# Four attention layers: two banks of sums in turn and a ring of two banks for the second self-attention layer

## The reference

```python
def _forward(x, encoder_out, norm_w, Wq, Wkv, Wqf, Wkf, Wwin, Wout):
    xn = rmsnorm(x, norm_w)
    q = (xn @ Wq).reshape(B, T_dec, H, hd)
    k, v = ...                       # (encoder_out @ Wkv): 77 tokens of context
    q_phi = taylor_feature_map(q @ Wqf)
    k_phi = taylor_feature_map(k @ Wkf)
    kv_state = jnp.einsum('bshf,bshd->bhfd', k_phi, v)
    linear_out = jnp.einsum('bthf,bhfd->bthd', q_phi, kv_state)
    normalizer = jnp.einsum('bthf,bhf->bth', q_phi, k_phi.sum(axis=1))[..., None]
    linear_out = linear_out / (normalizer + EPS_DEN)
    kv_win = (xn @ Wwin).reshape(B, T_dec, 2, H, hd)
    scores = jnp.einsum('bthd,bshd->bhts', q, k_win) * (1.0 / math.sqrt(hd))
    allowed = (j <= i) & (j >= i - WINDOW)
    probs = softmax(where(allowed, scores, min))
    window_out = jnp.einsum('bhts,bshd->bthd', probs, v_win)
    return residual + concatenate([linear_out, window_out]) @ Wout
```

## Time and profile before

| | us |
|---|---|
| Median of 3 runs | 2349.58 |
| Lowest and highest run | 2344.32, 2349.96 |
| Profiled execution, its own time | 2344.72 |
| Its span in the trace | 2343.0 |
| TensorE busy (share of the span) | 2060.6 (88%) |
| TensorE's weight loads | 1351.1 (58%) |
| VectorE busy | 1409.6 (60%) |
| ScalarE busy | 1132.0 (48%) |
| GpSimd busy | 728.3 (31%) |

### The profile page before, as it was taken

One profiled execution on the slowest core, in us unless ns is written; L12 is line 12 of the kernel. 1 busy time (PEld: TensorE's weight loads), 2 busy tenths in 40 slices (PEclk: granted clock), 3 DMA queues, 4 the chain that ended last, 5 costly groups with the idle time before them and its releaser, 6 DMA issues. The chain is left out here.

```text
span 2343.0 us, 38173 instructions
## 1 busy us (share of the span) xinstructions
PE 2060.6 (88%) x14594; PEld 1351.1 (58%) x14594; DVE 1409.6 (60%) x3047; ACT 1132.0 (48%) x1675; POOL 728.3 (31%) x817
## 2 busy tenths in 40 slices
PE   4898999899998879887889898996989995899989
PEld 2333433343343268775565575664677773888989
DVE  5775776586678356635535454451577882656655
ACT  1255465555555756523434534362555553545444
POOL 2013114113213143311524426153110100555656
PEclk8799999999999989998999999999999996999999
DMA  6705404502530000036440805302222212000000
GB/s 129 144 6 108 57 1 75 88 8 51 91 72 1 1 14 1 10 90 89 112 58 29 141 1 122 48 2 79 81 82 95 82 42 72 6 14 13 12 14 19
DMA packets 77772, 126.65 MB, mean 54 GB/s; under 512 B 16652, under 2 KB 34828, under 8 KB 77584
## 3 DMA queue, kind: packets, MB, share of 16 engines
q1 hardware_dynamic: 74968, 122.63, 25.0%
q10 hardware_dynamic: 2624, 1.58, 0.2%
HBM read 93.59 MB, written 30.32 MB: 53 GB/s over the span
## 5 line engine op out<-in xcount | busy, mean ns | idle before, releaser
L1007 DVE TENSOR_REDUCE nmx_causal<-banks 128x1 f32<-128x333 f32 (+4 forms) x896 | 436.0, 537 | 174.9 <-PE banks L739 172.1
L893 ACT ACTIVATE probs_causal<-banks 128x1024 f32<-128x1024 f32 (+3 forms) x384 | 352.4, 952 | 283.0 <-PE banks L764 279.9
L739 PE MATMUL banks<-ks_causal,qs_causal 96*128 96x333 bf16 (+4 forms) x896 | 272.8, 342 | 11.8 <-DVE nmx_causal L1007 9.5
L670 POOL TENSOR_SCALAR_AFFINE_SELECT probs_window<-probs_window 128x512 f32<-128x512 f32 (+1 forms) x272 | 162.8, 605 | 306.7 <-ACT probs_window L893 296.2
L670 POOL TENSOR_SCALAR_AFFINE_SELECT probs_causal<-probs_causal 128x512 f32<-128x512 f32 x128 | 89.0, 696 | 510.4 <-ACT probs_causal L893 510.4
L764 PE MATMUL banks<-qs_causal,ks_causal 97*128 97x512 bf16 (+4 forms) x896 | 220.1, 343 | 28.1 <-DMA qs_causal<-nmT_causal 15.0
L1007 DVE TENSOR_REDUCE nmx_window<-banks 128x2 f32<-128x384 f32 (+2 forms) x320 | 140.5, 458 | 117.2 <-PE banks L739 115.5
L788 PE MATMUL banks<-probs_causal,v_causal 128*17 128x512 f32 (+4 forms) x1792 | 198.6, 516 | 0.0
L893 ACT ACTIVATE probs_window<-banks 128x768 f32<-128x768 f32 (+2 forms) x128 | 99.8, 783 | 129.3 <-PE banks L764 128.8
L739 PEld LDWEIGHTS banks<-ks_causal,qs_causal 96*128 96x128 bf16 x896 | 87.2, 100 | 111.8 <-DVE nmx_causal L1007 70.4
L737 PEld LDWEIGHTS banks<-below,identb 128*128 128x128 bf16 x512 | 50.3, 99 | 168.1 <-DVE nmx_causal L1007 116.9
(11 more groups left out here) (251 smaller groups left out, 4098.6 us busy)
## 6 DMA issues: line engine op xcount, KB each, us to landing
fs_masked<-in_fside SPq DMA_DIRECT2D x32, 616.0 KB, 3.7
ks_causal<-zk SPq DMA_DIRECT2D x96, 137.6 KB
ks_window<-zk SPq DMA_DIRECT2D x96, 137.6 KB
qs_causal<-zq SPq DMA_DIRECT2D x96, 128.0 KB
qs_window<-zq SPq DMA_DIRECT2D x96, 128.0 KB
zk<-parts_causal SPq DMA_DIRECT2D x24, 275.2 KB, 2.5
zk<-parts_window SPq DMA_DIRECT2D x24, 275.2 KB, 2.4
zq<-parts_causal SPq DMA_DIRECT2D x24, 256.0 KB, 4.6
```

The lines of the kernel that those rows point to most:

```text
L670: pool.affine_select(out=v, in_=v, compare_op=ALU.is_ge, fill=0.0, base=const, pattern=[[0, QH], [by_c, wd]], channel_multiplier=by_p).the ...
L739: ins = pe.matmul(bk[:, c:c + m], qs[q][0:KR, h, t * P:(t + 1) * P], ks[q][0:KR, h, key:key + m], start=cover is None, stop=True, skip_gro ...
L893: ins = act.activation(dst, src, ACT.Exp, scale=DH ** -0.5)
L1007: dve.tensor_reduce(dst, src, AX.X, ALU.max, negate=True).then_inc(emptied_v, 1)
```

## The change

The windowed layer gets two banks of sums, 6 and 7, used by its turns alternately; the causal layer keeps bank 6 alone. A turn's first multiply waits for the copy of the turn before the last. In return bank 7 leaves the ring for all tokens of layers 1 and 2: their ring has banks 0 and 1, and a fill waits for the fill two back. For the causal layer the ring stays 0, 1, 7. The class Ring now takes a function from token to banks, goes through each choice of banks by turn, and remembers for each fill the last user of its bank. VectorE clears both banks before the layer. On every engine the instructions keep their order; VectorE has one memset more.

```diff
     def __init__(self, banks, where, order, emptier, ready, done):
-        self.banks, self.where, self.emptier, self.ready = banks, where, emptier, ready
+        self.banks, self.ready, self.done = banks, ready, done
         tokens = [t for t in order if emptier(t)]
-        self.done = done
         self.at = {t: n for n, t in enumerate(tokens)}
-        count, self.counts = dict.fromkeys(done, 0), []
-        for t in tokens:
+        count, turn, last = dict.fromkeys(done, 0), {}, {}
+        self.counts, self.used, self.before = [], [], []
+        for n, t in enumerate(tokens):
             count[emptier(t)] += 1
             self.counts.append((done[emptier(t)], count[emptier(t)]))
+            choice = where(t)
+            bank = choice[turn.get(choice, 0) % len(choice)]
+            turn[choice] = turn.get(choice, 0) + 1
+            self.used.append(bank)
+            self.before.append(last.get(bank))
+            last[bank] = n
...
     def wait_free(self, pe, token):
-        n = self.at[token] - len(self.where)
-        if n >= 0:
+        n = self.before[self.at[token]]
+        if n is not None:
             pe.wait_ge(*self.counts[n])
...
-PAIRS, OUT = (2, 4), 6
+PAIRS, SUMS = (2, 4), {True: (6,), False: (6, 7)}
...
+    sums_of = lambda n: SUMS[first][n % len(SUMS[first])]
...
+                out = sums_of(turn_number[b, q, c])
                 if s == 0:
-                    n = turn_number[b, q, c]
-                    if n:
-                        pe.wait_ge(out_copied, n)
+                    n = turn_number[b, q, c] - len(SUMS[first])
+                    if n >= 0:
+                        pe.wait_ge(out_copied, n + 1)
                     else:
-                        pe.wait_ge(cleared, 2)
+                        pe.wait_ge(cleared, 1 + len(SUMS[first]))
...
-                        ins = pe.matmul(banks[32 * h:32 * h + DH + 1, OUT, query:query + n],
+                        ins = pe.matmul(banks[32 * h:32 * h + DH + 1, out, query:query + n],
...
-                act.activation(oT[:, k % 2, :], banks[:, OUT, :], ACT.Copy).then_inc(out_copied, 1)
+                act.activation(oT[:, k % 2, :], banks[:, sums_of(k), :], ACT.Copy).then_inc(out_copied, 1)
...
-                dve.memset(banks[:, OUT, :], 0.0).then_inc(cleared, 1)
+                for bank in SUMS[first]:
+                    dve.memset(banks[:, bank, :], 0.0).then_inc(cleared, 1)
...
-    shared = Ring(banks, (0, 1, 7), order, emptied_by, sem("ring_ready"), {"v": sem("emptied_v"), "s": sem("emptied_s")})
+    shared = Ring(banks, lambda token: (0, 1) if token[0] else (0, 1, 7), order, emptied_by, sem("ring_ready"), {"v": sem("emptied_v"), "s": sem("emptied_s")})
```

More of the change, by code:

```diff
@@ L394, in __init__ @@
     def __init__(self, banks, where, order, emptier, ready, done):
-        self.banks, self.where, self.emptier, self.ready = banks, where, emptier, ready
+        self.banks, self.ready, self.done = banks, ready, done
         tokens = [t for t in order if emptier(t)]
-        self.done = done
         self.at = {t: n for n, t in enumerate(tokens)}
-        count, self.counts = dict.fromkeys(done, 0), []
-        for t in tokens:
+        count, turn, last = dict.fromkeys(done, 0), {}, {}
+        self.counts, self.used, self.before = [], [], []
+        for n, t in enumerate(tokens):
             count[emptier(t)] += 1
             self.counts.append((done[emptier(t)], count[emptier(t)]))
+            choice = where(t)
[4 more added lines that the diff above has]
+            last[bank] = n
     def bank(self, token):
-        return self.banks[:, self.where[self.at[token] % len(self.where)], :]
+        return self.banks[:, self.used[self.at[token]], :]
     def filled(self, token):
@@ L941, in step @@
             if token == ("ring", 0, 0, 0, 0):
-                dve.wait_ge(cleared, 2)
+                dve.wait_ge(cleared, 1 + len(SUMS[first]))
             if emptier(token) == "v":
@@ L1240, in front_layers @@
     names = [lambda s, tag=tag: sem(f"{s}_{tag}") for tag in ("causal", "ff", "window")]
-    shared = Ring(banks, (0, 1, 7), order, emptied_by, sem("ring_ready"), {"v": sem("emptied_v"), "s": sem("emptied_s")})
+    shared = Ring(banks, lambda token: (0, 1) if token[0] else (0, 1, 7), order, emptied_by, sem("ring_ready"), {"v": sem("emptied_v"), "s": sem("emptied_s")})
     rings = [Own(shared, n) for n in range(3)]
     products_of = lambda token: {"up": "s", "down": "v"}.get(token[0])
-    own_banks = Ring(banks, (2, 3, 4, 5, 6), of(1), products_of, sem("product_ready"),
+    own_banks = Ring(banks, lambda token: (2, 3, 4, 5, 6), of(1), products_of, sem("product_ready"),
                      {"v": sem("product_emptied_v"), "s": sem("product_emptied_s")})
```

## The result

The change made the kernel slower: 2405.88 us against 2349.77 (medians of 4 runs each, 2402.98 to 2407.23 and 2344.32 to 2351.80). The ratio is 1.0233, 95% interval 1.0214 to 1.0252. That is 56 us lost where +32.5 was summed up and 2380 forecast, and it lies above the range's 2398.

A forecast was written before the change was run, and what follows sets the result against it. TensorE was taken as the layer's bound. On the profiled 2344.7 us, -15 + 13 + 18 + 2 + 2.5 + 12 = +32.5 gave 2377; half of the median's 5 us excess on top made 2380 us, range 2352 to 2398.

The forecast's parts named there:

- Part 1: Second bank of sums in the windowed layer's attention: TensorE no longer waits for ScalarE's copy, -15 us, bounds 10 to 19.6.
- The cap by the transposes: Attention turns: where transposes of the copied sums follow a stall, at most 0.55 us of it comes back.
- Value stages: Ring of two where values are projected: each next value block waits 0.41 us, 3.3 us a batch, 13 us for four.
- Feed-forward layer: Ring of two at 820 to 1050 us: none of 33 fills begins before the bank two back is free, 0 us.
- Output stages: Ring of two: 18 us over the first three batches' output stages, 2 us in the last batch's.
- The three places of one passage: First three output stages: waits of 0.59, 0.41 and 0.26 us add up to 1.26 us a passage, five passages a stage.
- The stage of maxima alone: 1055 to 1065 us, once: about 0.1 us more for each of 20 fills, 2.5 us, between 0 and 3.3.
- Attention stages: Ring of two: late fills cost 12 us, 3 a batch, bounds 0 and 19.4; TensorE's idle time absorbs part.
- the walk: Fill-by-fill count of delays with two ring banks, no idle time taken off; 19.4 us in the attention stages.
- Rival 4: Slower by more, 2395 us and up: walk's full cost of 57, gain only 10; lower clock can add; chance 0.15.
- Two banks enough: Rival 2: the ring of two costs nothing, only the second bank of sums acts, 2330 or 2325 us; chance 0.08.
- Cancel: Rival 3: the gain of the second bank and the ring's loss cancel, 2344 to 2355 us; chance 0.15.

The follow-up runs named there:

- e1: The changed kernel with only one bank of sums everywhere, the ring of two kept in the feed-forward and windowed layers: 2417.70 us, ratio 1.0297 to the kernel before.
- e3: Kernel before, with two alternating banks of sums only in each batch's last five turns and a ring of two only there: 2343.59 us, ratio 0.9973.
- e7: The kernel of e3 measured again on another chip with more runs: 2349.02 us, ratio 0.9991 to the kernel before.
- e4: e1 plus filler multiplies with unused results before three waits in each of three batches: 2411.49 us, ratio 1.0263 to the kernel before.
- e5: Kernel before, one bank of sums, ring of two only in the second group of heads of the first three batches: 2381.84 us, ratio 1.0128.

## Why the prediction was right or wrong

**Direction: right, and for the stated reason.** The ring of two costs more than the second bank gives.

**Part 1: right.** 15 us forecast, 12 by the medians of e1 and the change, 15 by their traces, of which 9 are idle time; the rest is most likely in part the clock. The cap by the transposes holds: their row of waits for the copy grew from 3.2 to 8.5 us. Waits for GpSimd's masks, which I had not priced, took 3 us more (5.5 against 2.5).

**Value stages: right.** 13 forecast, 13.3 measured, 3.3 a stage, with the step of 0.41 us seen: value blocks follow each other after 1.64 us (1250.07 to 1251.71), and after 1.23 before.

**Feed-forward layer: put at 0, some 3 us measured.** "None of its 33 fills begins before the bank two back is free" left out the place where the ring changes. The first layer's last fills use three banks in turn and the feed-forward layer's first already two, and there the bank that comes next needn't be the one used two fills back. Shown is the wait of 2.11 us at 817.71; that the order of banks makes it is my reading.

**Output stages: right in kind, two sizes off.** In the first three 18 was forecast and 13.6 came (13.6 to 16.2 in the kernels with a ring of two there). The three places of one passage don't all bind each time: of 15 passages, 12 show a wait of a block of maxima for ScalarE's copy (5.3 us), 12 one for VectorE's addition (2.7), and 3 one of the transpose for the maxima (1.1). In the last one 2 was forecast and 4.3 came. All of the 4.3 is counted as busy time, and the lower level lasts 6.1 us longer there; e3 and e7, with three ring banks in this stage, are 1.4 longer at 3.4 us more of it. That is a term I didn't have. Its first product, eight multiplies that take 1.89 to 1.97 us before, takes 3.75 at a granted clock of 0.50:

```profile
1656.13:1659.88 3.75, 3.75 (x10) 2.93 (x10) 0.00 (x0) 0.60 (x1) 0.00 (x0) 0.50 0.00 0
```

**The stage of maxima alone:** 2.5 forecast, 3.1 after, 1.6 to 2.6 in the other kernels with a ring of two there. The size is right, but TensorE stands at the lower level for 9.9 us more there and is busy 2.9 us more, so the trace doesn't show whether the mechanism I had or the clock makes the 3.1.

**Attention stages: the step that failed.** 12 us forecast and 40 measured with a ring of two alone (e1), of which 29.6 lie in the three stretches with projections. Outside of these it is 10.4 us, which the 12 would have covered. Inside, the prediction said that "part of the delay falls into waits that end when they end, such as one where VectorE is held for 2.60 us by a cast". It took such long holds by a third engine as time that would swallow delays. At the place that it named, in the third group, that was so: TensorE's longest wait there is 2.16 us before and 2.84 after, and all four third groups lose only 0.8 us by idle time (the other 4.2 of their 5.1 are busy time, with 10.2 us more of the lower level). In the second group the holds are the opposite. A hold of a bank by ScalarE that waits for GpSimd is itself a bank taken out of the ring, for 4.5 us. With three banks two were left to go on with; with two only one is, and TensorE stops at once. And the end of the hold isn't fixed: it moves along with TensorE. From the start of the held fill to ScalarE's copy of it, it is 5.76 us before (1282.69 to 1288.45) and 5.57 after (1312.67 to 1318.24), while the stretch has grown. By the recorded times alone the fill behind it lacked 3.9 us (1285.13 to 1289.05), in one of three such stretches; the whole walk of the prediction came to 19.4 us for all sixteen groups, and even this upper bound is under the 29.6 of the three. How much of it the walk gave to these fills is not on record.

**The clock: named, not priced, and expected elsewhere.** Rival 4 looked for the lower level behind the new gaps of the value and output stages. The value stages have 0.5 us more of it, the first three output stages 3.0. Where it came is the projection stretches (20.5), the third groups (10.2), the stage of maxima (9.9) and the last output stage (6.1). e4 puts its price in the projection stretches at about 10 us, for 27 us less of the lower level than in e1.

**Against the sum:** 32.5 forecast, 60.7 in the trace. The attention stages are 28 of the difference, the last output stage 2, the part ahead of the layer 3 (the ring of the feed-forward layer), the output stages -4, what follows the layer -2. The 2.5 us put on top for the median was harmless.

**The rivals.** Two banks enough: fell. The stages with TensorE full cost what they must, and for the rule of the Trainium skill (Perfetto Trace Analysis, Optimizing Tensor Performance, Matmuls) that groups should rotate through different banks, e5 shows that two banks do rotate and still cost 30 us in three stretches, where with three the held copies stop TensorE for 2.0 us each. How many banks it takes follows here from how long one stays full, which the rule doesn't speak of. Cancel: fell. Slower by more was the case that came, from 2391 up, but its sum reached it by other terms: a smaller gain and the whole walk, where the held fills and the clock behind them made it. The range ended where it did because its top took the walk's 19.4 us for all attention stages, and because I left the clock, which I had said could add to it, out of its top.

**Still open.** How the busy time outside the projection stretches divides between the clock and waits counted as busy, and the few us that may lie in two banks of sums in the last turns only.

## What to carry to other kernels

Before taking a buffer out of a ring, look for the fill that stays full longest, not for the mean fill, and ask who its emptying engine is waiting for: if that is a third engine, count this buffer as gone for that time and see whether the rest can feed the multiplies. Don't let idle time of the recorded run swallow a delay unless what ends it is independent of the delayed engine. Where a walk yields idle stretches of some us on TensorE, price the multiplies behind them at the lower clock level as well, from a row of the same multiplies at that level. Where a ring changes its number of banks, look at that place by itself.

## What the runs showed of the hardware

The same four multiplies of 128x512 float32 took 1.98 us at a granted clock of 1.00 and 3.68 us at 0.54, right behind an idle stretch of 3.72 us; with 0.95 us of idle time before them instead (e4), 1.98. Filling an idle stretch of TensorE with multiplies that nobody needs gave back 10 us in three stretches.

At the same granted clock of 1.00, a value stage with waits in it shows 1.65 us more of busy TensorE for the same multiplies (11.94 against 10.29).

The hand-over from an emptying to the next fill's multiply measured 0.05 us in the value stage with two banks (1251.66 to 1251.71), and behind ScalarE's copies 0.06 with two (1318.24 + 0.60 to 1318.90) as with three (1288.45 + 0.60 to 1289.11).
